# Power iterations of a four-layer conv stack on one Trainium2 core: turning a row into a column by one-column matmuls instead of transposes

## The reference, cut to what matters

```python
u = x.reshape(B, C, N)                       # N = 1024, x group-normalised
gram = jnp.einsum('bci,bcj->bij', u, u)
fdist = jnp.sqrt(jnp.maximum(sq[:, :, None] + sq[:, None, :] - 2.0 * gram, 0.0) + EPS)
T = fdist * D[None]                          # D: fixed Gaussian of the pixels' distance
T = T / jnp.maximum(jnp.sum(T, axis=1, keepdims=True), EPS)
def step(p, _):                              # 20 times
    p = jnp.einsum('bij,bj->bi', T, p)
    p = p / jnp.maximum(jnp.sum(p, axis=1, keepdims=True), EPS)
    return (p, None)
...
x = x + x * p.reshape(B, 1, H, W)
```

## Time and profile before

| | |
|---|---|
| median of three runs | 14203.45 us (14203.05 to 14216.56) |
| the profiled execution | 14197.43 us |
| its span, first to last instruction | 14195.5 us |
| eight power stages | together about 1140 us of the span |

### The profile page before, as it was taken

How to read it: one execution, slowest core, us unless ns; L and a number is a source line. 1 busy time by engine, 2 the same in 40 slices (tenths; PEclk the granted TensorE clock), 3 DMA queues, 4 the chain that set the end, 5 groups by cost and what they waited for, 6 DMA issues and landing times. The chain is left out here.

```text
span 14195.5 us, 99867 instructions
## 1 busy us (share of the span) xinstructions
PE 8487.1 (60%) x32544; PEld 4159.2 (29%) x32544; DVE 10033.0 (71%) x9864; ACT 2933.0 (21%) x4725; POOL 9517.5 (67%) x9221
## 2 busy tenths in 40 slices
PE   5783657346734666265734674466645567567777
PEld 3242224122413233132412232223322233233333
DVE  6756977598767976698758966697756977555543
ACT  2232113122212122121312131212202122001111
POOL 0005777777777777777777777777777667777740
PEclk7896778667866788577866787678877788888889
DMA  1012122311232123212231123212322113232210
GB/s 70 9 22 70 52 60 67 85 52 52 61 82 69 52 60 85 66 51 60 64 88 52 52 61 82 68 52 60 85 75 75 44 55 81 92 99 81 81 61 39
DMA packets 890426, 913.07 MB, mean 64 GB/s; under 512 B 692418, under 2 KB 702658, under 8 KB 880643
## 3 DMA queue, kind: packets, MB, share of 16 engines
q0 software_dynamic: 294912, 604.57, 15.2%
q1 hardware_dynamic: 594946, 301.65, 7.4%
HBM read 770.26 MB, written 135.28 MB: 64 GB/s over the span
## 5 line engine op out<-in xcount | busy, mean ns | idle before, releaser
L124 POOL DMA_INDIRECT gat<-corner_tables,idx x9216 | 9517.0, 1033 | 4149.1 <-issue 2773.8
L140 DVE TENSOR_TENSOR gat<-gat,wts 128x1152 f32<-128x1152 f32 x1024 | 1387.3, 1355 | 1658.2 <-DMA gat<-corner_tables,idx 1543.3
L144 DVE TENSOR_REDUCE dcn<-gat 128x32 f32<-128x1152 f32 x1024 | 2152.9, 2102 | 38.8
L766 PE MATMUL PS<-hc,ident 128*128 128x512 f32 (+2 forms) x4096 | 1989.2, 646 | 295.2 <-DVE hc L807 232.3
L830 DVE TENSOR_TENSOR_SCAN hs<-dA,PS 128x1024 f32<-128x1024 f32 x672 | 1532.2, 2280 | 46.6 <-ACT dA L783 18.6
L766 PEld LDWEIGHTS PS<-hc,ident 128*128 128x128 f32 x4096 | 1024.7, 283 | 931.1 <-issue 490.6
L1039 PE MATMUL PS<-ident,E 128*128 128x128 f32 x4096 | 613.0, 298 | 477.3 <-ACT ET L1108 246.9
L807 DVE TENSOR_TENSOR hc<-hs,PS 128x1024 f32<-128x1024 f32 x672 | 802.4, 1194 | 0.8 <-issue 0.8
L745 PE MATMUL PS<-bc1b,pick 96*128 96x512 bf16 x1024 | 406.3, 503 | 642.7 <-DVE hc L807 642.6
L1118 ACT ACTIVATE E<-PS,nmax 128x1024 f32<-128x1024 f32 x512 | 570.0, 1113 | 1022.6 <-DVE nmax L1175 808.4
L745 PE MATMUL PS<-bc1f,pick 96*128 96x512 bf16 x1024 | 403.1, 500 | 617.4 <-DVE hc L807 617.2
(11 more groups left out here) (241 smaller groups left out, 10840.2 us busy)
## 6 DMA issues: line engine op xcount, KB each, us to landing
gat<-corner_tables,idx POOLq DMA_INDIRECT x9216
corner_tables<-xp SPq DMA_DIRECT2D x1024, 64.0 KB, 2.2
D<-in_dist_dram SPq DMA_DIRECT2D x8, 4096.0 KB, 13.5
wqkv<-in_qkv_w_dram SPq DMA_DIRECT2D x8, 3072.0 KB, 11.2
corner_tables<-gat SPq DMA_DIRECT2D x1, 17280.0 KB, 54.9
X<-in_x_dram SPq DMA_DIRECT2D x32, 512.0 KB, 6.0
w_in<-in_in_w_dram SPq DMA_DIRECT2D x16, 1024.0 KB, 7.1
w_c<-in_c_w_dram SPq DMA_DIRECT2D x16, 1024.0 KB
```

Source lines behind the costliest of these rows:

```text
L124: nc.gpsimd.indirect_dma_start(bd.gat[n % self.NG][:, k * 4 * CG:(k + 1) * 4 * CG], None, bd.rows, bass.IndirectOffsetOnAxis(ap=bd.idx[:, ...
L140: nc.vector.tensor_tensor(v, v, wv, ALU.mult).then_inc(self.prod, 1)
L144: nc.vector.tensor_reduce(bd.dcn[m % 2][:, g * CG:(g + 1) * CG], gat[:].rearrange("p (k c) -> p c k", c=CG), AX.X, ALU.add).then_inc(self. ...
L766: mm = nc.tensor.matmul(PS[:, p.ybank(d, h), 0:p.hl], self.ident[:], src[:, j, h * p.hl:(h + 1) * p.hl], start=(c == 0 and j == 0), stop=( ...
```

## The change

The eight transposes of step 4 become eight matmuls with `row`'s 128 columns as weights and one column of ones as the moving operand. Each sums over all 128 partitions, of which four hold the partial sums and the others zeros, so that its result is already a pixel's total. The eight results are eight columns of PSUM bank 4, and step 5 goes away: L1700 and L1703 (and their forms for k = 0) read PSUM themselves.

```diff
-            mw = self.sb(ctx, "mw", [P, PT])
...
                         for i in range(PT):
                             if i % (PT // 2) == 0:
                                 pe.wait_ge((row0_out, row1_out)[i // (PT // 2)], k + 1)
-                            mm = nc.tensor.transpose(PS[:, 4 + i // 4, (i % 4) * P:(i % 4 + 1) * P],
-                                                     row[:, i * P:(i + 1) * P], self.ident[:])
+                            mm = nc.tensor.matmul(PS[:, 4, i:i + 1], row[:, i * P:(i + 1) * P], self.ones[:, 0:1],
+                                                  start=True, stop=True)
                         mm.then_inc(col_done, 1)
...
-                        o.step(nc.vector.tensor_reduce(
-                            mw[:], PS[:, 4:6, :].rearrange("p a (m j c) -> p (a m) j c", j=4, c=32)[:, :, :, 0],
-                            AX.X, ALU.add))
-
+                        mw = PS[:, 4, 0:PT]
                         if k:
                             last = rs[:, (k - 1) % 2:(k - 1) % 2 + 1]
-                            nc.vector.scalar_tensor_tensor(out=wp[:, :, 0], in0=mw[:], scalar=last,
+                            nc.vector.scalar_tensor_tensor(out=wp[:, :, 0], in0=mw, scalar=last,
                                                            in1=rinv[:], op0=ALU.mult, op1=ALU.mult)\
                                 .then_inc(w_ready, 1)
-                            nc.vector.tensor_scalar(raw[:], mw[:], last, None, ALU.mult)\
+                            nc.vector.tensor_scalar(raw[:], mw, last, None, ALU.mult)\
                                 .then_inc(raw_ready, 1)
```

More of the change, by code:

```diff
@@ L1692, in _ @@
                         dve.wait_ge(col_done, k + 1)
-                        o.step(nc.vector.tensor_reduce(
-                            mw[:], PS[:, 4:6, :].rearrange("p a (m j c) -> p (a m) j c", j=4, c=32)[:, :, :, 0],
-                            AX.X, ALU.add))
+                        mw = PS[:, 4, 0:PT]
                         if k:
                             last = rs[:, (k - 1) % 2:(k - 1) % 2 + 1]
-                            nc.vector.scalar_tensor_tensor(out=wp[:, :, 0], in0=mw[:], scalar=last,
+                            nc.vector.scalar_tensor_tensor(out=wp[:, :, 0], in0=mw, scalar=last,
                                                            in1=rinv[:], op0=ALU.mult, op1=ALU.mult)\
                                 .then_inc(w_ready, 1)
-                            nc.vector.tensor_scalar(raw[:], mw[:], last, None, ALU.mult)\
+                            nc.vector.tensor_scalar(raw[:], mw, last, None, ALU.mult)\
                                 .then_inc(raw_ready, 1)
                         else:
-                            nc.vector.tensor_tensor(wp[:, :, 0], mw[:], rinv[:], ALU.mult).then_inc(w_ready, 1)
-                            nc.vector.tensor_copy(raw[:], mw[:]).then_inc(raw_ready, 1)
+                            nc.vector.tensor_tensor(wp[:, :, 0], mw, rinv[:], ALU.mult).then_inc(w_ready, 1)
+                            nc.vector.tensor_copy(raw[:], mw).then_inc(raw_ready, 1)
                         spread()
```

## The result

The changed kernel takes 14263.21 us (median of six runs, 14253.86 to 14272.68) against 14204.99 us for six runs of the kernel before: a ratio of 1.0041, with a 95% interval of 1.0030 to 1.0051. It is slower by about 58 us. The profiled execution took 14258.42 us, its span is 14256.2 us, 60.7 more than before. All lines of the changed kernel named here stand one or four lower than in the kernel before: the product is L1645, the turning matmuls L1655, `wp` L1696.

The account below looks back on a forecast made before the run. A ring of PE, ACT and DVE waiting for each other bounds stages 7 and 8 fully, the gather ends stages 3 to 6. 60 + 23 + 3 + 22.7 = +109 us on 14203.45: about 14310 us, range 14222 to 14365.

Parts of the forecast that it names:

- Passes: PE, each power-stage iteration: sixteen one-column fp32 passes take 1.94 us where eight transposes took 1.09, +0.85 us.
- Rival C: Loads of the sixteen passes: they follow at half the distance, passes take 1.09 us, total 14194 us; chance 0.05.
- DVE's step: DVE, each iteration: the removed sum saves 0.22 us, and reading PSUM instead of SBUF costs nothing.
- A fall's price: Passes and next product after a clock fall: +0.6 us and +1.7 us, together 2.3 us.
- How many falls: Pauses between products: the clock falls in three of eight, 7.5 times in twenty, +17 us per stage.
- the ring: Power-stage iteration: product, ACT's copy, transposes, DVE's sum and `wp` wait in turn; one turn grows from 6.07 to 6.70 us.
- rival A: Power stages: turns lengthen and the clock falls in a good part of the pauses; 14260 to 14360 us, chance 0.66.
- The mechanism: Undisturbed power stage: longer turns add 12.6 us and clock falls 17 us, about +30 us.
- rival B: Power stages: turns lengthen but the clock holds; +30 us, 14234 us (14222 to 14246), chance 0.29.
- Stages 3 to 6: Power stages beside the gather: its waits are used up, then +5.8 us each, +23 us together.
- Stages 1 and 2: First two power stages: +22.7 us each; nearly all given back behind stage 1, leaving +3, and kept behind stage 2.
- The rule of the Trainium skill: Pauses between products: transposes don't count for the clock like matmuls, so they protected nothing and it could hold; no size.

Follow-up runs that it names:

- e8_copy: The changed kernel, but DVE copies the eight totals to SBUF first; one run, 181 us above the median before on its chip.
- e1_wide: The changed kernel, but each matmul's moving operand is 128 columns of ones instead of one; 14234.65 us, 1.0027 of the kernel before.
- e6_delay: The kernel before, transposes kept, with three dependent 128x8 DVE copies to an unused tile added behind the sum; one run, 14231.22 us.

## Why the prediction was right, point by point

- **Passes** (+0.85 us a turn, from L1578's sixteen one-column passes): 1.95 against 1.94. The term holds, and it held although those loads have one row and the new ones 128. Rival C is out.
- **DVE's step** (-0.22): 6.70 us a turn as worked out, and putting a step of that kind back costs 0.20. `wp` takes 0.23 us from PSUM as it did from SBUF.
- **A fall's price** (2.3 us): 4.5 for a pair, so the mean holds, but partly by luck. The working was +0.6 for the passes and +1.7 for the product. The first fall of a pair costs 0.35 and 2.7, the second nothing and 1.4; in e8_copy a fall costs 1.4 to 1.7. (The products begun at half clock go up to 6.58 us, not 6.44 as the prediction says: stage 4.)
- **How many falls** (7.5 per stage, from three of eight pauses before gram): this is the term that was mis-sized. There were 4 that hit the turns, in stage 7 one more at the start, and in stages 3 to 6 one behind the last turn. Eight looks at a pause of another stage were made into a chance per pause; in the ring the pauses come at fixed distances and the falls in pairs, two pairs per stage in both traces of the changed kernel. Nor was three of eight a property of the pause before gram: in the trace after, all eight groups take 1.94 us. The working for four falls under rival A gave +58 us, which is what was measured, and stage by stage it fits: 44 against 44.6 for stages 7 and 8, 0 against 1, 14 against 11.6 for stage 2, and 0 against 3.4 for stage 1. 14310 us was 47 us too high, nearly all of it this one term carried through the stages.
- **The mechanism**: the direction needs no fall, since the longer ring alone gives rival B's +30 us, and e1_wide, with no fall in stages 7 and 8, is 36 us slower. That the falls belong to the new passes is shown by e6_delay, at the same pause and turn: 9 slow products beside the first in eight stages with transposes, 33 with one-column passes.
- **Stages 3 to 6** (+23): +1, because with four falls the ring needs less than the gather does. DVE's waits fell from 22.4 to 6.2 us, so 6 us of the cover is left; with 7.5 falls it would have gone.
- **Stages 1 and 2** (+22.7 each, given back behind stage 1): +11.7 and +11.6, and 8.3 of the first given back, not nearly all. The waits behind stage 1 fell by 18 us, more than what came back. What of them had been beside other work wasn't measured.
- **The rule of the Trainium skill** (TensorE: Matmul & The Clock Gate, Part 4: transposes don't count for the clock as matmuls do) spoke for rival B. The runs go against what the prediction drew from it, that the transposes protected nothing: with eight fp32 transposes in a pause of 3.04 us there are one or two slow products per stage beside the first, with one-column passes in 3.06 us four or five.

## What to carry to other kernels

Here the loads set the price of a matmul with one column: sixteen fp32 passes took 1.95 us, and 2.05 us with 128 columns each. So "fewer steps" on VectorE (0.2 us) were paid for with more time on TensorE (0.85 us). On a ring in which the engines wait for each other, look at what TensorE does in the pause as well as how long it is; e1_wide's useless columns made the turn 0.10 us longer and the stage 7 to 10 us shorter, though its new turn may have a part in that. And ask for each stage what ends last there: the same longer ring cost 20 us or more in stages 7 and 8, where nothing ran beside it, 12 in stages 1 and 2, where 9 us of waits took up part, and nothing in stages 3 to 6, where the gather already set the end.

## What the runs showed of the hardware that was not expected

- The falls of the clock are regular: pairs 58 to 65 us apart in the changed kernel, at the same turns within one or two from stage to stage, and 6 to 10 falls instead of 4 or 5 when the bare pause grows from 3.06 to 3.26 us. What decides the turn wasn't tested.
- Eight bf16 loads of 128 columns take 0.26 us, eight fp32 transposes' loads 0.85 us; sixteen fp32 passes are not twice but more than five times as long as eight bf16 passes (1.95 against 0.35 us).
- On three of the chips every kernel of this kind took about 20% longer, with clean stages 7 and 8. Why wasn't settled. The change cost more there in the one run of it (165 us; 181 and 256 us with the copy), and the bf16 row gained 47 to 91 us, where stages 7 and 8 account for 38.
